# Edge features as two float32r parts, and the weight ring filled behind that stage

## The chip, the cores and the metric

The kernel runs on one core of one Trainium2 chip. The metric is the device time of one execution in microseconds. It stands at 4577.11 us, the median of three runs (4573.23 to 4581.51 us).

## The reference, cut to what matters

The program is four blocks over 512 nodes of 768 features and 8704 edges: in each a graph layer, an attention-like mixer and a feed-forward layer, and between them layer norms and residual sums. Only the first graph layer reads the edge features, a table of 8704 rows of 256 float32 values:

```python
edge_proj = edge_features @ We.T + be
for l in range(3):
    msgs = nodes[src] + nodes[dst] + edge_proj
    agg = jax.ops.segment_sum(msgs, dst, num_segments=512)
```

A sum over the edges of a node commutes with the product by `We`. So the kernel needs, for each node, the sum of the feature rows of the edges that end in it: a 256 x 512 matrix, `edge_sum_t`, at float32 accuracy.

## The kernel before

**The stage that the change touches.** Edges lie 128 on the partitions, in 68 chunks (`EC`). `edge_sum_t` is made by TensorE as a product of a chunk's features (128 edges x 128 features, the stationary operand) with a selection matrix (128 edges x 512 nodes, a one where the edge ends in the node), accumulated over all chunks in two PSUM banks, one for each half of the features. To keep float32 accuracy with bf16 operands each feature is split exactly into three bf16 parts, `feat_bits[...][:, 0..2, :]`: the value rounded to bf16, the rounded rest, and the rest of that.

Four chunks form a batch (`BATCHES` = 17). For a batch n:

- ScalarE writes part 0 (`first_bits`, L1440) and part 1 (L1446) and waits for VectorE's first subtraction between them (L1445).
- VectorE subtracts part 0 from the features (L2127, into `feat_rest`), builds the four selection matrices with one comparison each (L2132, a float16 iota against the edge's target, into `feat_hot`), and subtracts part 1 from the rest to give part 2 (L2134). It counts `onehot_ready` up by four there.
- TensorE waits for that count (L678) and runs 4 chunks x 2 halves x 3 parts = 24 matmuls of 512 columns (L683), and counts `onehot_used` up once a chunk.

`feat_bits` has three buffers, reused in order. `feat_hot` has two sets of four: the comparisons of batch n wait until batch n-2 is used (L2130, from n = 2). So VectorE is at most one batch ahead.

**Work put in between.** The first layer norm (`ln0`) runs inside this stage. On VectorE, behind the batch's last subtraction: one addition of two node chunks in batches 0 to 3 (L2042), small tables of edge kinds in batch 5 (L2107 to L2111), after a wait for TensorE's sum two centring steps in each of batches 6, 7 and 8 (L2144), a reciprocal in batch 13 (L2148), and two multiplications in each of batches 14, 15 and 16 (L2152). On TensorE: two float32 matmuls behind batch 5 (`norm_sums`) and six behind batch 10 (`square_sums`). On ScalarE: two squares in each of batches 7, 8 and 9 and a square root in batch 12. The order is the order of the code on each engine.

**What follows.** TensorE counts edges by kind in 6 groups of 34 chunks (L702, L703, L709, bf16), then does transposes (L539), degree sums (L541) and the first linear layer, which is the first reader of the weight ring.

**The SyncE queue** issues, in order: the node features and a column table, a wait until the second part of the edge features is in (L337), six weight tiles of 512 KB into the ring (L339), a wait for the fourth part of the edge features (L387), and `moe_pack` twice (L356 to L361), 34 transfers from HBM to HBM that repack expert weights for much later stages. Then come the ring's further tiles (L352), each waiting until its slot is free. ScalarE's queue issues the edges and the edge features, in four parts of 8, 16, 20 and 24 chunks.

The ring lies at `WR_`, 24 KB a partition. The buffers of the feature stage lie elsewhere, at `E_`, `D_`, `F_` and `T_`.

Of the kernel before, what the change touches and what calls it, by code (L numbers as in the profile page):

```python
# [23 lines left out]
N, D, P = 512, 768, 128  # L24
E, EC = 8704, 8704 // 128
# [28 lines left out]
BATCHES = EC // 4  # L54
# [63 lines left out]
def program(nc, io, tables):  # L118
    f32, bf16, f16, i32 = mybir.dt.float32, mybir.dt.bfloat16, mybir.dt.float16, mybir.dt.int32
    ALU, ACT, AX = mybir.AluOpType, mybir.ActivationFunctionType, mybir.AxisListType  # L120
    ctx = ExitStack()
    with ctx:
        def sb(name, shape, dt=f32):
            return ctx.enter_context(nc.sbuf_tensor(name, list(shape), dt))

        def sem(name):
            return ctx.enter_context(nc.semaphore(name))
# [2 lines left out]
        KB = 256  # L130
        CNT, A_, B_, C_, D_, XN_, T_, QK_, PQ_, XT_, WR_, E_, F_, END = (
            0, 32, 44, 56, 68, 80, 92, 108, 116, 124, 136, 160, 172, 184)
        mem = sb("mem", [P, END * KB])

        def area(kb, a, b, c=None, rows=P):
            size = a * b * (c or 1)
            v = mem[0:rows, int(kb * KB):int(kb * KB) + size]
            if c is None:
                return v.rearrange("p (a b) -> p a b", a=a)
            return v.rearrange("p (a b c) -> p a b c", a=a, b=b)  # L140
# [18 lines left out]
        edge_i = area(QK_ + 4, 4, EC).bitcast(i32)  # L159
        edge_f = area(QK_ + 5.25, 6, EC)  # L160
        feats = area(CNT, EC, 256)
        feat_hot = area(E_, 8, N // 2).bitcast(bf16)
        feat_bits = [area(kb, 3, 2 * 256).bitcast(bf16) for kb in (E_ + 8, D_, D_ + 6)]
        feat_rest = [area(kb, 4, 256) for kb in (F_ + 8, T_ + 12)]
        onehot_a = area(CNT + 12, AHEAD, N // 2).bitcast(bf16)
        onehot_b = area(A_, AHEAD, N // 2).bitcast(bf16)
        edge_sum_t = area(PQ_ + 4, 2, N)
# [84 lines left out]
        bank_full, bank_free, tile_free, x_tile_free, agg_done, act_done, dve_done, pool_done = (tally[n] for n in tally)  # L252
# [4 lines left out]
        feat_in = [sem(f"feat_in{i}") for i in range(4)]  # L257
        onehot_ready, onehot_used = sem("onehot_ready"), sem("onehot_used")
# [75 lines left out]
        def _(sp):  # L334
            sp.dma_start(XT, io["xT"]).then_inc(x_in, 16)
            sp.dma_start(cols[:, :], io["cols"]).then_inc(cols_in, 16)
            sp.wait_ge(feat_in[1], 16)  # L337
            for s in range(RING):
                sp.dma_start(ring[:, s, :], io["weights"][s]).then_inc(w_in[s], 16)  # L339

# [191 lines left out]
        def _(pe):  # L532
# [83 lines left out]
            def square_sums(label):  # L616
                for k in range(KC):
                    pe.wait_ge(act_done.sem, act_done.at((label, "sq", k)))
                    ins = mm(bank[6][:, :], ones[:, :], sq[:, k, :], k == 0, k == KC - 1, k == KC - 1)
                ins.then_inc(agg_done.sem, agg_done.tick((label, "var")))  # L620
# [56 lines left out]
            for n in range(BATCHES):  # L677
                pe.wait_ge(onehot_ready, 4 * n + 4)  # L678
                for b in range(4):
                    for f in range(2):  # L680
                        for part in range(3):
                            at = b * 256 + f * P
                            ins = nc.tensor.matmul(bank[4 + f][:, :], feat_bits[n % 3][:, part, at:at + P], feat_hot[:, n % 2 * 4 + b, :],  # L683
                                                   start=n == 0 and b == 0 and part == 0, stop=n == BATCHES - 1 and b == 3 and part == 2)
                    ins.then_inc(onehot_used, 1)
                if n == 5:
                    norm_sums("ln0", XT, lambda k: None)
                elif n == 10:
                    square_sums("ln0")
            for p in range(len(PACKED)):  # L690
                for g, (start, stop) in enumerate(GROUPS):
                    n = len(GROUPS) * p + g
# [11 lines left out]
                    for chunk in range(start, stop):  # L704
                        done = EC * p + chunk
                        a, b = onehot_a[:, done % AHEAD, :], onehot_b[:, done % AHEAD, :]
# [660 lines left out]
        def _(act):  # L1367
# [67 lines left out]
            def first_bits(n):  # L1435
                if n in [start // 4 for start, _ in FEAT_PARTS]:
                    act.wait_ge(feat_in[[start // 4 for start, _ in FEAT_PARTS].index(n)], 16)
                if n >= 3:
                    act.wait_ge(onehot_used, 4 * (n - 2))
                nc.scalar.activation(feat_bits[n % 3][:, 0, :], feats[:, 4 * n:4 * n + 4, :].rearrange("p a f -> p (a f)"),  # L1440
                                     ACT.Identity).then_inc(act_done.sem, act_done.tick(("first_bits", n)))

            first_bits(0)
            for n in range(BATCHES):
                act.wait_ge(dve_done.sem, dve_done.at(("feat_rest", n)))  # L1445
                nc.scalar.activation(feat_bits[n % 3][:, 1, :], feat_rest[n % 2].rearrange("p a f -> p (a f)"), ACT.Identity).then_inc(  # L1446
                    act_done.sem, act_done.tick(("middle_bits", n)))
                if n + 1 < BATCHES:
                    first_bits(n + 1)
                if n in (7, 8, 9):  # L1450
                    for k in (2 * n - 14, 2 * n - 13):
                        act.wait_ge(dve_done.sem, dve_done.at(("ln0", "d", k)))
                        nc.scalar.activation(sq[:, k, :], XN[:, k, :], ACT.Square).then_inc(act_done.sem, act_done.tick(("ln0", "sq", k)))
                elif n == 12:
                    act.wait_ge(agg_done.sem, agg_done.at(("ln0", "var")))
                    nc.scalar.activation(rstd[:, :], bank[6][:, :], ACT.Sqrt, scale=1.0 / D, bias=eps_col[:, :]).then_inc(
                        act_done.sem, act_done.tick(("ln0", "std")))
# [577 lines left out]
        def _(dve):  # L2035
            v = nc.vector

            def add_up(label, x, m):

                if 1 <= m < KC - 1:  # L2040
                    dve.wait_ge(dve_done.sem, dve_done.now())
                    v.tensor_tensor(mean[:, :], x[:, 0, :] if m == 1 else mean[:, :], x[:, m, :], ALU.add).then_inc(  # L2042
                        dve_done.sem, dve_done.tick((label, "part")))
# [71 lines left out]
            def key(n, c):  # L2115
                if isinstance(c, int):
                    return edge_f[:, n, c:c + 1]
                return edge_f[:, n, bass.ds(c, 1)]


            def flat(x):
                return x.rearrange("p a f -> p (a f)")

            for n in range(BATCHES):
                bits, rest = feat_bits[n % 3], flat(feat_rest[n % 2])
                dve.wait_ge(act_done.sem, act_done.at(("first_bits", n)))
                v.tensor_tensor(rest, flat(feats[:, 4 * n:4 * n + 4, :]), bits[:, 0, :], ALU.subtract).then_inc(  # L2127
                    dve_done.sem, dve_done.tick(("feat_rest", n)))
                if n >= 2:
                    dve.wait_ge(onehot_used, 4 * (n - 1))  # L2130
                for b in range(4):
                    v.tensor_scalar(feat_hot[:, n % 2 * 4 + b, :], iota_h, key(1, 4 * n + b), None, ALU.is_equal)  # L2132
                dve.wait_ge(act_done.sem, act_done.at(("middle_bits", n)))
                v.tensor_tensor(bits[:, 2, :], rest, bits[:, 1, :], ALU.subtract).then_inc(onehot_ready, 4)  # L2134
                if n == 0:
                    dve.wait_ge(x_in, 16)
                if n < 4:
                    add_up("ln0", XT, n + 1)
                elif n == 5:
                    edge_kinds()  # L2140
                elif n in (6, 7, 8):
                    dve.wait_ge(agg_done.sem, agg_done.at(("ln0", "sum")))
                    for k in (2 * n - 12, 2 * n - 11):
                        v.scalar_tensor_tensor(XN[:, k, :], bank[7][:, :], -1.0 / D, XT[:, k, :], ALU.mult, ALU.add).then_inc(  # L2144
                            dve_done.sem, dve_done.tick(("ln0", "d", k)))
                elif n == 13:
                    dve.wait_ge(act_done.sem, act_done.at(("ln0", "std")))
                    v.reciprocal(rstd[:, :], rstd[:, :]).then_inc(dve_done.sem, dve_done.tick("ln0_rstd"))  # L2148
                elif n > 13:
                    dve.wait_ge(dve_done.sem, dve_done.at("ln0_rstd"))  # L2150
                    for k in (2 * n - 28, 2 * n - 27):
                        v.tensor_tensor(XN[:, k, :], XN[:, k, :], rstd[:, :], ALU.mult).then_inc(dve_done.sem, dve_done.tick(("ln0", k)))  # L2152
# [28 lines left out]
            for p in range(len(PACKED)):  # L2181
                a, b_ = (0, 1) if p < 2 else (1, 0)
# [714 lines left out]
```

## Time and profile before

| | us |
|---|---|
| median of three runs | 4577.11 |
| lowest, highest | 4573.23, 4581.51 |
| span of the profiled execution, first to last instruction | 4586.8 |
| TensorE busy in it | 4400.9 (96%) |
| VectorE busy | 1028.0 (22%) |
| ScalarE busy | 1005.9 (22%) |

The profile gives no time of the profiled execution other than its span; that span lies 9.7 us above the median of the runs, 0.2%. Busy TensorE does not mean TensorE at its peak: matmuls are pipelined and their ends are modelled, so the distance from one start to the next is what a matmul costs, not its duration. A float32 matmul shows as two records. In the chain of waits, pieces with the name of a line are work on that line, and "issue" is time in which the engine waited for nothing that the profile shows.

### The profile page before, as it was taken

What the parts mean: (1) busy time and instruction counts of PE and PEld (TensorE: products, weight loads), DVE (VectorE), ACT (ScalarE), POOL (GpSimd) and SP (SyncE); (2) the same over time, 40 slices, a digit from 0 to 9 for tenths busy, and PEclk for the clock granted to TensorE, in tenths of its full rate; (3) what the DMA queues carried; (4) which work ended last, traced back from release to release, by engine and by line L of the source; (5) the groups of instructions that cost most, each with busy time, mean ns of one, the idle gap of its engine ahead of it and who ended that gap; (6) DMA issues with size and microseconds to landing.
All of it is one profiled execution on the core that took longest, in us unless ns stands there. A gap on an engine that the chain in (4) does not pass through costs nothing.

```text
span 4586.8 us, 37555 instructions
## 1 busy us (share of the span) xinstructions
PE 4400.9 (96%) x15153; PEld 1974.8 (43%) x15153; DVE 1028.0 (22%) x1909; ACT 1005.9 (22%) x1830; POOL 90.1 (2%) x169
## 2 busy tenths in 40 slices
PE   8999999999999998989999999999999999999998
PEld 3444444444445544444444444444444433433333
DVE  6871111212321325113300000023541000000000
ACT  3121122324214336222210101012621000110000
POOL 1000000000000000000000000000000000000000
PEclk9999999999999998999999999999899999999999
DMA  9513222111361120103203030355128999999998
GB/s 322 164 65 93 81 74 92 60 59 56 155 273 55 51 78 1 55 28 119 69 28 102 21 101 23 101 214 223 42 98 355 410 422 423 413 424 408 414 412 357
DMA packets 128791, 795.79 MB, mean 173 GB/s; under 512 B 13950, under 2 KB 26542, under 8 KB 82172
## 3 DMA queue, kind: packets, MB, share of 16 engines
q1 hardware_dynamic: 116892, 728.07, 42.2%
q0 software_dynamic: 9280, 45.81, 2.6%
q10 hardware_dynamic: 2464, 19.67, 1.1%
q8 instruction: 117, 1.92, 0.2%
q14 instruction: 38, 0.31, 0.0%
HBM read 774.47 MB, written 56.83 MB: 181 GB/s over the span
## 4 chain that ended last, share of the span: by engine, by line
PE 87%; DMA 5%; ACT 3%; DVE 3%; issue 1%; POOL 0%; SPq 0%; ACTq 0%; DVEq 0%; POOLq 0%
PE bank L541 78%; DMA mem<-in_experts 4%; PE bank L709 4%; PE bank L539 3%; PE bank L683 2%; ACT mem L1722 1%; ACT mem L1743 0%; ACT mem L1888 0%; DVE mem L2411 0%; DVE mem L2077 0%; DVE mem L2407 0%; ACT mem L1381 0%; ACT mem L1758 0%; DMA mem<-moe_up 0%; DMA mem<-moe_bias 0%
## 5 line engine op out<-in xcount | busy, mean ns | idle before, releaser
L541 PE MATMUL bank<-mem 128*128 128x512 f32 (+5 forms) x11160 | 3539.0, 557 | 51.5 <-DMA mem<-in_experts 25.1
L541 PEld LDWEIGHTS bank<-mem 128*128 128x128 f32 (+3 forms) x11160 | 1486.4, 167 | 2022.6 <-issue 1904.2
L539 PE MATMUL bank<-ident,mem 128*128 128x128 f32 (+2 forms) x1484 | 225.1, 303 | 73.1 <-ACT mem L1915 13.4
L539 PEld LDWEIGHTS bank<-ident,mem 128*128 128x128 f32 (+2 forms) x1484 | 188.5, 156 | 161.9 <-issue 87.8
L1381 ACT ACTIVATE mem<-bank 128x512 f32<-128x512 f32 x171 | 101.4, 596 | 511.3 <-PE bank L541 506.5
L1381 ACT ACTIVATE mem<-bank,cols 128x512 f32<-128x512 f32 (+1 forms) x82 | 56.2, 686 | 688.4 <-PE bank L541 688.4
L709 PE MATMUL bank<-mem 128*128 128x512 bf16 x816 | 177.2, 379 | 0.0
L2716 DVE TENSOR_TENSOR mem<-mem,EV 128x512 f32<-128x512 f32 x48 | 33.2, 692 | 549.2 <-ACT EV L1989 549.2
L541 PE MATMUL bank<-mem,ones 128*128 128x512 f32 (+1 forms) x314 | 141.9, 621 | 13.5 <-ACT mem L1415 7.2
L2694 DVE TENSOR_TENSOR mem<-mem,bank 128x512 f32<-128x512 f32 x48 | 33.0, 688 | 459.7 <-PE bank L541 459.7
L709 PEld LDWEIGHTS bank<-mem 128*128 128x128 bf16 x816 | 79.3, 98 | 97.5 <-issue 1.3
L2598 DVE COPY mem<-mem 128x512 f32<-128x512 f32 x12 | 4.2, 420 | 485.6 <-ACT mem L1381 485.6
L683 PE MATMUL bank<-mem 128*128 128x512 bf16 x408 | 90.9, 386 | 15.6 <-DVE mem L2134 15.6
L1989 ACT ACTIVATE EV<-bank 128x512 f32<-128x512 f32 x48 | 28.7, 597 | 310.9 <-PE bank L541 310.9
L1985 ACT ACTIVATE mem<-bank 128x512 f32<-128x512 f32 x48 | 28.7, 597 | 300.5 <-PE bank L541 300.5
L2090 DVE TENSOR_TENSOR mem<-mem,EV 128x512 f32<-128x512 f32 x30 | 20.8, 692 | 325.7 <-ACT EV L1392 325.7
L541 PEld LDWEIGHTS bank<-mem,ones 128*128 128x128 f32 (+1 forms) x314 | 55.7, 189 | 88.3 <-issue 56.6
L2187 DVE TENSOR_SCALAR mem<-mem 128x512 bf16<-128x512 f16 x204 | 82.5, 404 | 0.0
L1392 ACT ACTIVATE EV<-bank,cols 128x512 f32<-128x512 f32 x30 | 20.6, 687 | 279.1 <-PE bank L541 279.1
L2186 DVE TENSOR_SCALAR mem<-mem 128x512 bf16<-128x512 f16 x204 | 70.8, 347 | 29.6 <-PE bank L709 23.3
L1996 ACT ACTIVATE mem<-bank,pair_score 128x384 f32<-128x384 f32 x16 | 9.3, 581 | 275.1 <-PE bank L541 275.1
L2407 DVE SCALAR_TENSOR_TENSOR mem<-mem 128x2048 f32<-128x2048 f32 x27 | 61.8, 2287 | 33.8 <-ACT mem L1722 33.8
(364 smaller groups left out, 2147.9 us busy)
## 6 DMA issues: line engine op xcount, KB each, us to landing
mem<-in_experts SPq DMA_DIRECT2D x282, 1536.0 KB, 11.9
mem<-in_weights SPq DMA_DIRECT2D x329, 512.0 KB, 3.6
mem<-moe_up SPq DMA_DIRECT2D x30, 1152.0 KB, 9.0
mem<-moe_down SPq DMA_DIRECT2D x30, 1152.0 KB, 10.2
moe_up<-in_weights SPq DMA_DIRECT2D x16, 1152.0 KB
moe_down<-in_weights SPq DMA_DIRECT2D x16, 1152.0 KB
mem<-in_weights POOLq DMA_DIRECT2D x36, 384.0 KB, 7.8
mem<-in_experts ACTq DMA_DIRECT2D x6, 1536.0 KB, 15.3
```

Source lines behind the costliest of these rows:

```text
L539: ins = nc.tensor.transpose(out, lhsT, ident[0:lhsT.shape[0], 0:lhsT.shape[0]])
L541: ins = nc.tensor.matmul(out, lhsT, rhs, start=start, stop=stop)
L683: ins = nc.tensor.matmul(bank[4 + f][:, :], feat_bits[n % 3][:, part, at:at + P], feat_hot[:, n % 2 * 4 + b, :], start=n == 0 and b == 0 a ...
L709: ins = nc.tensor.matmul(banks[c][:, :], a[:, c * P:(c + 1) * P], b, start=False, stop=chunk == stop - 1)
L1381: nc.scalar.activation(dst(m), src[0:width, :], func, scale=scale, **how).then_inc(bank_free.sem, bank_free.tick((label, m)))
L1722: ins = nc.scalar.activation(scores[:, buf, t, :], src[:, :], ACT.Identity, bias=stat[:, at:at + 1])
L1985: nc.scalar.activation(x_hidden[:, b, :], src[:, :], ACT.Silu).then_inc(bank_free.sem, bank_free.tick((kind, p, b)))
L2186: v.tensor_scalar(onehot_a[:, done % AHEAD, :], iota_h, key(a, c), None, ALU.is_equal)
L2187: v.tensor_scalar(onehot_b[:, done % AHEAD, :], iota_h, key(b_, c), key(2 + p, c), ALU.is_equal, ALU.mult).then_inc(onehot_ready, 1)
L2407: v.scalar_tensor_tensor(wide, wide, 0.2, wide, ALU.mult, ALU.max).then_inc(dve_done.sem, dve_done.tick())
L2694: v.tensor_tensor(XT[:, m, :], XT[:, m, :], bank[7][:, :], ALU.add).then_inc(dve_done.sem, dve_done.tick(("experts_x", p, m)))
L2716: v.tensor_tensor(x_hidden[:, u // 2, :], x_hidden[:, u // 2, :], EV[:, u // 2 % 2, :], ALU.mult).then_inc(dve_done.sem, dve_done.tick(("x ...
```

## The change

The features are split into two float32r parts in place of three bf16 parts: the value rounded to float32r by ScalarE, and what is left of it, written by VectorE. The selection matrices are float32r too. All operands of L683 are then 4 bytes wide, and a batch has 16 matmuls. ScalarE's second conversion, VectorE's first subtraction and the buffer `feat_rest` go. The wider buffers take the ring's place (`WR_`, 24 KB) beside `E_` and `D_`, so the SyncE queue waits, before it fills the ring, until the whole stage is used (`onehot_used` at 68) and no longer for the second part of the features. All that SyncE issues behind the ring comes behind this wait as well.

```diff
-        feat_hot = area(E_, 8, N // 2).bitcast(bf16)
-        feat_bits = [area(kb, 3, 2 * 256).bitcast(bf16) for kb in (E_ + 8, D_, D_ + 6)]
-        feat_rest = [area(kb, 4, 256) for kb in (F_ + 8, T_ + 12)]
+        feat_hot = rounded("feat_hot", WR_, (8, N))
+        feat_bits = [rounded(f"feat_bits{n}", kb, (2, 4 * 256)) for n, kb in enumerate((WR_ + 16, E_, D_))]
...
-            sp.wait_ge(feat_in[1], 16)
+            sp.wait_ge(onehot_used, EC)
             for s in range(RING):
                 sp.dma_start(ring[:, s, :], io["weights"][s]).then_inc(w_in[s], 16)
...
-                        for part in range(3):
+                        for part in range(2):
                             at = b * 256 + f * P
                             ins = nc.tensor.matmul(bank[4 + f][:, :], feat_bits[n % 3][:, part, at:at + P], feat_hot[:, n % 2 * 4 + b, :],
...
-            first_bits(0)
             for n in range(BATCHES):
-                act.wait_ge(dve_done.sem, dve_done.at(("feat_rest", n)))
-                nc.scalar.activation(feat_bits[n % 3][:, 1, :], feat_rest[n % 2].rearrange("p a f -> p (a f)"), ACT.Identity).then_inc(
-                    act_done.sem, act_done.tick(("middle_bits", n)))
-                if n + 1 < BATCHES:
-                    first_bits(n + 1)
+                first_bits(n)
...
             for n in range(BATCHES):
-                bits, rest = feat_bits[n % 3], flat(feat_rest[n % 2])
-                dve.wait_ge(act_done.sem, act_done.at(("first_bits", n)))
-                v.tensor_tensor(rest, flat(feats[:, 4 * n:4 * n + 4, :]), bits[:, 0, :], ALU.subtract).then_inc(
-                    dve_done.sem, dve_done.tick(("feat_rest", n)))
+                bits = feat_bits[n % 3]
                 if n >= 2:
                     dve.wait_ge(onehot_used, 4 * (n - 1))
                 for b in range(4):
                     v.tensor_scalar(feat_hot[:, n % 2 * 4 + b, :], iota_h, key(1, 4 * n + b), None, ALU.is_equal)
-                dve.wait_ge(act_done.sem, act_done.at(("middle_bits", n)))
-                v.tensor_tensor(bits[:, 2, :], rest, bits[:, 1, :], ALU.subtract).then_inc(onehot_ready, 4)
+                dve.wait_ge(act_done.sem, act_done.at(("first_bits", n)))
+                v.tensor_tensor(bits[:, 1, :], flat(feats[:, 4 * n:4 * n + 4, :]), bits[:, 0, :], ALU.subtract).then_inc(onehot_ready, 4)
```

`rounded` is a new helper that places a float32r tensor at a fixed offset in the same memory.

## Rows read from the trace of the kernel before

**Rows 1.** The page: the span, and the chain that ended last, by engine and line.
```profile
span 4586.8 us, 37555 instructions
...
PE 87%; DMA 5%; ACT 3%; DVE 3%; issue 1%; POOL 0%; SPq 0%; ACTq 0%; DVEq 0%; POOLq 0%
PE bank L541 78%; DMA mem<-in_experts 4%; PE bank L709 4%; PE bank L539 3%; PE bank L683 2%; ACT mem L1722 1%; ACT mem L1743 0%; ACT mem L1888 0%; DVE mem L2411 0%; DVE mem L2077 0%; DVE mem L2407 0%; ACT mem L1381 0%; ACT mem L1758 0%; DMA
```

**Rows 2.** The chain in order of time, 0 to 330 us: start, length, what.
```profile
10.64 1.06 ACT mem L1440
...
11.80 1.23 DVE mem L2127
13.03 1.15 DVE mem L2132 x4
...
14.22 1.24 DVE mem L2134
...
15.59 33.55 PE bank L683 x144
49.13 1.72 PE bank L541 x4
50.85 25.90 PE bank L683 x120
76.75 5.15 PE bank L541 x12
81.90 31.08 PE bank L683 x144
112.98 0.32 PE bank L702
...
300.70 1.75 PE bank L539 x16
302.45 13.73 PE bank L541 x32
```

**Rows 3.** Groups of instructions, 0 to 114 us: busy, mean ns, idle before.
```profile
L683 PE MATMUL bank<-mem 128*128 128x512 bf16 x408 | 90.9, 386 | 15.6 <-DVE mem L2134 15.6
```

**Rows 4.** Timeline inside the stage, TensorE and VectorE: start, length, what.
```profile
50.69 9.66 PE L683 MATMUL bank<-mem 128*128 128x512 bf16 x44
50.89 1.29 DVE L2144 SCALAR_TENSOR_TENSOR mem<-bank,mem 128x512 f32<-128x512 f32 x2 [4.46 <-PE bank L541]
52.10 1.21 DVE L2127 TENSOR_TENSOR mem<-mem 128x1024 f32<-128x1024 f32 x1
...
71.61 1.14 DVE L2132 TENSOR_SCALAR mem<-mem 128x512 bf16<-128x512 f16 x4 [1.67 <-PE bank L683]
72.67 1.22 DVE L2134 TENSOR_TENSOR mem<-mem 128x1024 bf16<-128x1024 f32 x1
...
89.31 3.35 DVE L2148 RECIPROCAL rstd<-rstd 128x512 f32<-128x512 f32 x1
92.57 1.16 DVE L2127 TENSOR_TENSOR mem<-mem 128x1024 f32<-128x1024 f32 x1
```

**Rows 5.** Timeline of VectorE around 814 us, a float32 operation with a per-partition operand.
```profile
814.44 1.67 DVE L2240 TENSOR_SCALAR mem<-mem,stat 128x512 f32<-128x512 f32 x4
```

**Rows 6.** Timeline of SyncE's queue, 0 to 175 us.
```profile
15.78 2.81 SPq L339 DMA_DIRECT2D mem<-in_weights  x6
...
35.30 0.73 SPq L359 DMA_DIRECT2D moe_up<-in_weights  x1
...
168.94 1.25 SPq L361 DMA_DIRECT2D moe_bias<-in_weights  x1
```

**Rows 7.** Windows: us, length, busy PE, PEld, DVE, ACT, POOL, granted clock, DMA share, GB/s.
```profile
180.00:185.00 5.00, 5.00 (x25) 2.26 (x24) 3.95 (x12) 2.21 (x2) 0.00 (x0) 1.00 0.11 41
...
3216.00:3220.00 4.00, 1.26 (x10) 0.84 (x9) 3.54 (x6) 4.00 (x12) 0.00 (x0) 1.00 0.42 131
3220.00:3224.00 4.00, 4.00 (x10) 1.80 (x10) 2.90 (x15) 4.00 (x9) 0.00 (x0) 0.75 0.00 0
```

More of the change, by code:

```diff
@@ L132, in program, with rounded @@
             0, 32, 44, 56, 68, 80, 92, 108, 116, 124, 136, 160, 172, 184)
+        mem_at = -(-nc.sbuf_base // 32) * 32
         mem = sb("mem", [P, END * KB])
+        f32r = mybir.dt.float32r
+        def rounded(name, kb, shape, rows=P):
+            return nc.alloc_sbuf_tensor_at(name, [rows] + list(shape), f32r, offset=mem_at + int(kb * 1024))
         def area(kb, a, b, c=None, rows=P):
@@ L680, in _ @@
                     for f in range(2):
-                        for part in range(3):
+                        for part in range(2):
                             at = b * 256 + f * P
                             ins = nc.tensor.matmul(bank[4 + f][:, :], feat_bits[n % 3][:, part, at:at + P], feat_hot[:, n % 2 * 4 + b, :],
-                                                   start=n == 0 and b == 0 and part == 0, stop=n == BATCHES - 1 and b == 3 and part == 2)
+                                                   start=n == 0 and b == 0 and part == 0, stop=n == BATCHES - 1 and b == 3 and part == 1)
                     ins.then_inc(onehot_used, 1)
```

## The prediction

> **What bounds the kernel now.** I read the page first, for the chain that ended last: TensorE holds 87% of it, and the lines of the feature stage little of that, 2% for L683 [rows 1]. So the change can move a few tens of microseconds of 4577 and no more, and the stage has to be read by itself. Second, the chain in order of time over the first 330 us [rows 2]. The reader is to see that it has one head (ScalarE's first conversion, VectorE's subtraction, four comparisons, second subtraction) and from 15.59 us on only TensorE: 408 matmuls of L683 in three pieces, with 4 and 12 records of the layer norm between them, and at 112.98 the counting stage, without a piece of another engine. Third, the groups: L683's only idle time, 15.6 us, is the head [rows 3]. The stage is bound by TensorE's stream, and VectorE and ScalarE hide behind it. Fourth, VectorE's and SyncE's timelines, for what the change turns into a bound [rows 4 to 6].
>
> **Part by part.**
>
> *Matmuls.* The last two pieces give 25.90/120 and 31.08/144, both 0.2158 us from one matmul to the next [rows 2]. The first piece has 144 as well and took 33.55, so the slow start of TensorE costs 2.47; I keep that. The change drops 136 of 408 matmuls. If a float32r matmul of 512 columns costs what a bf16 one does, 136 x 0.2158 = 29.35 us go.
>
> No float32r matmul is in the trace. Below, its price is bounded by the bf16 one: as many columns pass through. Above, the nearest row is float32: 32 records in 13.73 us, 0.429 each, two records to a matmul, so 0.858 a matmul [rows 2]. That is four times 0.2146, the pace of a bf16 matmul. Four is what the products of two halves by two halves make, and an operand that is not cut in halves needs one. So I take 0.2158. It also says that 4-byte operands can be streamed at that pace. The weight load is no obstacle: float32 records of 128 columns follow each other by 1.75/16 = 0.109 us with a load each [rows 2], so a 4-byte load fits within 0.216. The ends for the range are 0.2158 and 0.429 (0.858 for the extreme that float32r runs as float32).
>
> The Trainium skill (FP8 and Floating Point Precision, TensorE Precision Notes) says that true float32 takes four passes and that there is a reduced form which reads 4-byte values and truncates them. Its four passes agree with 0.858 = 4 x 0.2146; that the reduced form takes one pass it does not say in so many words, and no run so far shows it. By one pass the stage's matmuls would be an estimated 272 x 0.2146 = 58.4 us, by four 233 us.
>
> *The head.* Before, the first matmul starts at 15.59, after L1440, L2127, L2132 and L2134 in a row. After the change the comparisons stand ahead of the wait for ScalarE and need only the edges, which VectorE has long before 10.64. Left are L1440 and one subtraction, which starts at 11.80 where L2127 did, and takes 1.23; with the 0.14 from 15.45 (14.22 plus 1.23, as I read its end) to 15.59 TensorE starts at 13.17. That is 2.42 us earlier.
>
> *VectorE for a batch.* Comparisons before: from 71.61 to the subtraction's start at 72.67, 1.06 for four, 0.265 each [rows 4]. Their output becomes 4 bytes wide. The nearest row is the float32 operation with a per-partition operand: four in 1.67, the last one lasting 0.48, so (1.67 - 0.48)/3 = 0.397 each, 1.59 for four [rows 5]. Bounds: 0.265 if the width costs nothing; above, 1.22 for 1024 elements of L2127 against about 0.69 for 512 says 0.53 more for 512 elements at one a cycle, and 0.397 had 256 steps' worth, so 0.397 + 0.267 = 0.66 each, 2.66 for four, if a 2-byte source with a 4-byte result falls to one element a step. I take 1.59: the row has the result's width and the source costs less. The subtraction stays at 1.22; its rows with bf16 and with float32 results are alike (L2134 and L2127) [rows 4].
>
> The Trainium skill (VectorE: DVE Perf Modes, The perf-mode tier table) speaks against the change here: 4 elements a cycle only for 2-byte operands in SBUF, 2 for float32. That is 128 against 256 cycles, an estimated 0.133 us more for each comparison; the rows' 0.397 - 0.265 = 0.132 agrees.
>
> VectorE may begin batch n+1 when batch n-1 is used, which is when TensorE starts batch n. From there: 0.20 us until VectorE runs (TensorE's next matmul started at 50.69, VectorE's L2144, which waited for the one before, at 50.89), 1.59, 1.22, and 0.14 to TensorE: 3.15 [rows 4]. TensorE's batch is 16 x 0.2158 = 3.45. In plain batches 0.30 us are to spare; before, VectorE idled 1.67 in front of the comparisons at 71.61.
>
> Now the layer norm's work, which was hidden in that reserve. It stands between two batches on VectorE, and the next instruction starts 0.09 before the last ends. One addition (0.60, half of the 1.21 for two in [rows 4]) starts 0.23 before TensorE's batch (0.14 and 0.09) and lets the comparisons begin at 0.37 in place of 0.20; the reserve covers that, four times. The kinds' tables of batch 5 fall beside the two float32 matmuls. Then:
> - batch 6: VectorE waits for the sum, 0.20, and centres two chunks, 1.21 (50.89 to 52.10), then 1.59 + 1.22 + 0.14 = 4.36 against 3.45: a stall of 0.91.
> - batches 7 and 8: -0.23 + 1.21 + 1.59 + 1.22 + 0.14 = 3.93: 0.48 each.
> - batch 13: the reciprocal, 3.26 (89.31 to 92.57): -0.23 + 3.26 + 2.95 = 5.98, less 3.45, less the 0.30 that VectorE is ahead: 2.23.
> - batches 14 and 15: two multiplications, priced like the centring steps: 0.48 each. Batch 16's lie behind the last batch.
> The stalls sum to 5.06 us. ScalarE now has one conversion of 1.06 for a batch and at most 1.2 of squares beside it, in 3.45 to 4.4: it is not late.
>
> *Sum.* TensorE starts at 13.17; 272 x 0.2158 = 58.70; slow start 2.47; layer norm 1.72 + 5.15; stalls 5.06: the stage ends at 86.3 instead of 112.98. The saving is 29.35 + 2.42 - 5.06 = 26.7 us. From 112.98 to 316 the chain is TensorE alone, so it carries over whole.
>
> *SyncE.* The wait moves from 15.8 to about 86.3. Behind it queue the six ring tiles and the 34 transfers of `moe_pack`, whose wait for the features is then met. Issuing them took from 15.78 to 18.59 and from 35.30 to 170.19, 134.9 us [rows 6]; they would be issued by 86.3 + 2.8 + 134.9 = 224, and the transfers, which die out by 185, 15 us after the last issue [rows 7], by 239. The first reader of the ring is the linear layer, at 316 (302.45 plus 13.73) less 27 = 289, and SyncE's next tile waits for that layer [rows 2]: 50 us are left, and the ring itself is in by about 115 at the worst. The cost is nothing, and it would begin to cost only if the transfers took 1.4 times as long. The features lose a competitor: their last part, in by 35.3, is wanted in batch 11, at 62. That gains nothing either, since nothing waited for it.
>
> **The profiled execution and the median.** The sum is made against the span, 4586.8 - 26.7 = 4560.1. The profiled run lies 9.7 us above the median; I take the same saving off the median: 4577.1 - 26.7 = 4550.4 us.
>
> **Rivals.**
>
> *A, the forecast*, 4550: chance 0.68. Its own range is 4545 to 4558, from comparisons at 0.265 each (the stalls shrink to 1.5 us, 3.5 more saved) to a clock that falls in the 2.23 us stall. For the latter the trace has a case: after 4 us in which TensorE was busy for 1.26 the granted clock read 0.75 [rows 7]; at half speed a batch costs 3.45 more, and one or two would.
>
> *B, VectorE becomes the bound.* Comparisons at 0.66 each make 0.20 + 2.66 + 1.22 + 0.14 = 4.22 in a plain batch, 0.77 over TensorE's, and the extra work finds no reserve at all. By the same steps the stalls are 0.77 four times, 0.94 twice, 0.40, 1.58, 1.55 four times and 3.60, 16.7 in place of 5.1. Saving 15.1: 4562. For it: a float16 source with a 4-byte result is not in the trace. Against it: no row of a dense comparison or copy ran at one element a step. Chance 0.11.
>
> *C, slower: a float32r matmul costs one float32 record, 0.429.* It decides at 0.333: there 272 matmuls are as long as the old 408 (88.05) and the head's 2.42; the stalls vanish as TensorE slows. At 0.429 the matmuls take 116.7, nothing stalls (a batch is 6.9), and the saving is 88.05 - 116.7 + 2.42 = -26.2: 4603. For it: two records to a float32 matmul may mean that the hardware's unit for 4-byte operands is the record. Against it: the record has twice the time of a pass. The extreme, float32r run as float32, gives 88.05 - 233.4 + 2.42 = -142.9: 4720. Chance 0.09 for both, 0.02 of it the extreme: that is also the case in which the change doesn't do what it says.
>
> *D, the 4-byte weight load isn't hidden.* If a load of 0.109 [rows 2] were added to each matmul, 0.325 each, the matmuls take 88.3, without stalls, and the saving is 88.05 - 88.3 + 2.42 = 2.2: 4575. Against it: the float32 records of 512 columns keep 0.429, twice 0.2146, with a load each, so there it is hidden. Chance 0.06.
>
> *E, the gain is taken back behind the stage*: `moe_pack` beside the counting stage down to its end, late tiles, or another wait. Before, the same transfers ran beside this stage until 185 and no TensorE idle time stands there; a loss of half would give 4564. Chance 0.06.
>
> **Range and chances.** What one measurement tells from no change here is 0.2%, 9 us. Leaving out C (0.09), D (0.06) and a little of A's lower edge, the range is 4541 to 4569. Faster by over 0.2% (below 4568): A, B and E, 0.85. Within 0.2%: D, 0.06. Slower: C, 0.09.
>
> **What would show it.** L683 has 272 matmuls, one record each, 0.216 from start to start, and the last ends near 86. VectorE's four comparisons span about 1.6 to the subtraction. TensorE waits for the subtraction's line six times, 5.1 us in all, the longest 2.2 before batch 14. The counting stage is 187.7 long as before, and SyncE's last `moe_pack` issue is at about 221. I am wrong in the price if the distance is 0.3 or 0.43, wrong about VectorE if plain batches stall, and wrong about the carry-over if the stage ends at 86 and the whole does not follow.

## The result, and the profile after

| | before | after |
|---|---|---|
| median of the first comparison, us | 4579.24 | 4553.62 |
| ratio, 95% interval | | 0.9942 (0.9930 to 0.9954) |
| median of a second comparison, us | 4580.02 | 4554.53 |
| ratio, 95% interval | | 0.9941 (0.9928 to 0.9955) |
| span of the profiled execution, us | 4586.8 | 4550.0 |
| its own time, us | not given | 4551.79 |
| feature stage ends at, us | 112.98 | 88.51 |

The change makes the kernel faster by 25.6 us, where 26.7 were forecast. The spans of the two profiled executions lie 36.8 apart, which is more than the medians do: single executions of one kernel differ by some 12 us (4545.26 to 4557.60 after), so the question of where the time came from is answered in the stage and not by the spans.

The forecast was 4550.4 us, counted from a median before of 4577.11; the first comparison has 4579.24 before, so 2.1 of the 3.2 us between forecast and result come from the kernel before. The interval allows a saving of 21 to 32 us, so the whole's time can't tell 26.7 from the 24.5 that the stage shows below.

The page of the kernel after, its span and the chain that ended last:

```profile
span 4550.0 us, 37248 instructions
...
PE 87%; DMA 5%; ACT 3%; DVE 3%; issue 1%; SPq 0%; POOL 0%; ACTq 0%; DVEq 0%; POOLq 0%
PE bank L545 79%; DMA mem<-in_experts 4%; PE bank L713 4%; PE bank L543 3%; PE bank L687 1%; ACT mem L1721 1%; DMA mem<-moe_up 0%; ACT mem L1742 0%; ACT mem L1887 0%; DVE mem L2407 0%; DVE mem L2076 0%; DVE mem L2403 0%; ACT mem L1385 0%; ACT mem L1757 0%; DMA mem<-y_by_slot,slot_i 0%
```

TensorE holds 87% of the chain as it did [rows 1]. The share of the feature matmuls (L683 before, L687 now) has moved from 2% to 1%; the other large shares are the same within 1%. The chain over the first 300 us, as start, length and what:

```profile
10.66 1.07 ACT feat_bits L1444
11.82 1.24 DVE feat_bits L2130
...
13.19 24.42 PE bank L687 x96
37.61 1.73 PE bank L545 x4
...
39.97 0.68 DVE mem L2140
40.65 1.86 DVE feat_hot L2128 x4
42.51 1.14 DVE feat_bits L2130
43.70 15.42 PE bank L687 x64
59.12 5.15 PE bank L545 x12
64.27 3.69 PE bank L687 x16
...
70.79 0.85 DVE rstd L2144
...
73.97 1.30 DVE feat_hot L2128 x4
...
76.74 7.84 PE bank L687 x32
84.58 3.92 PE bank L687 x16
88.51 0.32 PE bank L706
...
276.23 1.75 PE bank L543 x16
277.98 13.73 PE bank L545 x32
```

Beside [rows 2] three things are to be seen. The head has lost a subtraction and the comparisons, and TensorE starts at 13.19, not at 15.59. VectorE's lines now stand inside the stage, where the chain was TensorE alone: at 40 us (centring, comparisons, subtraction) and at 71 us (the reciprocal and what follows it). And from the stage's end on nothing changed: 276.23 - 88.51 = 187.72, before 300.70 - 112.98 = 187.72, and the linear layer behind it still begins 15.5 us later. The stage gave 24.47 us and all of it arrived at the linear layer. The chains of both kernels have the same distance 480 us further on (first line before, second line after):

```profile
796.82 10.31 PE bank L541 x24
772.35 10.31 PE bank L545 x24
```

796.82 - 772.35 = 24.47. Behind 950 us it wanders in steps up and down, to 36.8 at the end of these two executions. These steps are not traced to a cause; the medians, 25.6 apart, don't keep them.

The groups of the stage (busy and mean ns of one, then idle before):

```profile
L687 PE MATMUL bank<-feat_hot,feat_bits 128*128 128x512 f32 x272 | 67.3, 406 | 15.4 <-DVE feat_bits L2130 15.4
L2128 DVE TENSOR_SCALAR feat_hot<-mem 128x512 fp32r<-128x512 f16 x68 | 28.9, 487 | 11.7 <-PE bank L687 11.5
```

and who waited for whom in the first 95 us (total, times, longest):

```profile
PEld bank L687 <- DVE feat_bits L2130: 4.7, 6, 2.0
```

A float32r matmul is one record, as forecast. TensorE's weight loads wait for the subtraction's line six times, 4.7 us in all, the longest 2.0; six times, 5.1 and 2.2 were forecast. This is idle time of the weight loads; what the matmuls lost is counted below.

The price of one matmul does not stand in its duration (406 ns, against 386 before [rows 3]) but in the distance of starts. The timeline of the weight loads up to the end of batch 5 (the last two loads of batch 2 and batches 3 to 5, where nothing stalls) has a row that gives it:

```profile
25.89 11.29 PEld L687 LDWEIGHTS bank<-feat_hot,feat_bits 128*128 128x128 f32 x50
```

The last of the 50 loads takes 0.195 (0.19 in the rows of single ones), so (11.29 - 0.195)/49 = 0.2264 us from one to the next. For bf16 it was 0.2158. VectorE's timeline, a plain batch and the reciprocal's:

```profile
30.39 1.68 DVE L2128 TENSOR_SCALAR feat_hot<-mem 128x512 fp32r<-128x512 f16 x4 [0.82 <-PE bank L687]
31.98 1.22 DVE L2130 TENSOR_TENSOR feat_bits<-mem,feat_bits 128x1024 fp32r<-128x1024 f32 x1
...
70.71 3.35 DVE L2144 RECIPROCAL rstd<-rstd 128x512 f32<-128x512 f32 x1
73.97 1.58 DVE L2128 TENSOR_SCALAR feat_hot<-mem 128x512 fp32r<-128x512 f16 x4
```

The comparisons take 31.98 - 30.39 = 1.59 to the subtraction, the value that was taken, and the 1.67 us that VectorE idled ahead of them [rows 4] are 0.82. SyncE's queue after:

```profile
88.54 2.81 SPq L343 DMA_DIRECT2D mem<-in_weights  x6
...
219.95 2.03 SPq L365 DMA_DIRECT2D moe_bias<-in_weights  x1
```

All that stood from 15.78 to 170.19 [rows 6] stands from 88.54 to 221.98. The linear layer, the ring's first reader, starts at 277.98 + 13.73 = 291.7, 70 us behind the last issue.

### The profile page after: what moved, and what is told of

Same layout as the page of the kernel before. It is cut to its first block, busy times and chain, and to the rows that moved or that the text cites. A ratio compares the mean times of both kernels' runs of the same rounds, so it can differ in the third digit from the quotient of the medians.

```text
span 4550.0 us, 37248 instructions
## 1 busy us (share of the span) xinstructions
PE 4371.0 (96%) x15017; PEld 1985.1 (44%) x15017; DVE 1017.1 (22%) x1892; ACT 990.1 (22%) x1813; POOL 92.0 (2%) x169
## 4 chain that ended last, share of the span: by engine, by line
PE 87%; DMA 5%; ACT 3%; DVE 3%; issue 1%; SPq 0%; POOL 0%; ACTq 0%; DVEq 0%; POOLq 0%
PE bank L545 79%; DMA mem<-in_experts 4%; PE bank L713 4%; PE bank L543 3%; PE bank L687 1%; ACT mem L1721 1%; DMA mem<-moe_up 0%; ACT mem L1742 0%; ACT mem L1887 0%; DVE mem L2407 0%; DVE mem L2076 0%; DVE mem L2403 0%; ACT mem L1385 0%; ACT mem L1757 0%; DMA mem<-y_by_slot,slot_i 0%
## 5 line engine op out<-in xcount | busy, mean ns | idle before, releaser
L713 PE MATMUL bank<-mem 128*128 128x512 bf16 x816 | 177.2, 379 | 0.0
L687 PE MATMUL bank<-feat_hot,feat_bits 128*128 128x512 f32 x272 | 67.3, 406 | 15.4 <-DVE feat_bits L2130 15.4
L2407 DVE CUSTOM_DVE_ANT_0 mem<-mem 128x512 f32<-128x512 f32 x108 | 68.3, 688 | 0.9
```

The lines of the kernel that those rows point to most:

```text
L713: ins = nc.tensor.matmul(banks[c][:, :], a[:, c * P:(c + 1) * P], b, start=False, stop=chunk == stop - 1)
L2407: v.tensor_tensor_reduce(out=s, in0=s, in1=cnt[r][:, t, :], scale=1.0, scalar=-3e38, op0=ALU.add, op1=ALU.max, accum_out=top[:, t, r:r + 1 ...
```

## The experiments

Each kernel below was compared with the kernel before on the same chip. Ahead of them, the account that they test, from the chain after: 88.51 - 13.19 = 75.32 us of stage are 272 x 0.2264 = 61.58 of matmuls, 6.88 of layer norm matmuls, a slow start of 24.42 - 96 x 0.2264 = 2.7, and 4.2 of stalls, which is what is left.

**The changed kernel again.** No edit.

> The changed kernel once more, beside the others on one chip. Theory: 0.994 of the kernel before (25 us less), the feature stage ends at 88.5. If the saving were chance between executions, it would lie under 9 us here.

Measured: 0.9941 (0.9928 to 0.9955), 4554.53 against 4580.02 us. Its stage ends at 88.54. The saving repeats.

**SyncE's wait alone.**

```diff
-            sp.wait_ge(feat_in[1], 16)
+            sp.wait_ge(onehot_used, EC)
             for s in range(RING):
```

> The kernel before with one part of the change alone: SyncE's wait ahead of the weight ring stands on the end of the feature stage, so the six ring tiles and the 34 repacking transfers are issued from about 113 us on. My theory (that move costs and gives nothing): the feature stage still ends at 113.0, the counting stage still takes 187.7, the last repacking transfer is issued at about 113 + 135 = 248, 70 us ahead of the first linear layer at 302 + 14 = 316, and the time is that of the kernel before within 0.1%. Rival (traffic out of the feature stage is what helps, or traffic in the counting stage is what hurts): the stage ends earlier than 113, or the counting stage takes more than 188, or the first linear layer waits, and the time moves by 3 us or more.

Measured: 1.0008 (0.9998 to 1.0017), 4582.08 against 4580.02 us. Its chain:

```profile
49.75 1.72 PE bank L541 x4
...
113.60 0.32 PE bank L702
...
301.32 1.75 PE bank L539 x16
```

The counting stage takes 301.32 - 113.60 = 187.72, to the hundredth what it took without the transfers moved into it. The stage ends 0.6 later, and that lies in its start: its first 144 matmuls took 49.75 - 15.56 = 34.19, of which 3.1 are a slow start, against 2.47 [rows 2]. SyncE's last repacking issue ends at 247.7, 69 us ahead of the linear layer at 316.8. So the move neither costs nor gives anything in the traced stages. The whole's interval doesn't exclude a cost of up to 0.17%, 8 us; nothing in the trace up to the linear layer shows one.

**Two parts, but bf16.** Leaves the third part of each feature out.

```diff
-        f32r = mybir.dt.float32r
+        f32r = mybir.dt.bfloat16
```

> The changed kernel with bf16 in the place of float32r, in features and selection matrices: two bf16 parts, so the third part of each feature is left out. All else is as in the changed kernel: 272 matmuls, the same order, the same waits. It takes away the two things that a 4-byte operand costs. Theory: a matmul goes back from 0.2266 to 0.2158 us from start to start (2.9 us in all), the four comparisons from 1.59 to 1.06, so that of 4.3 us of stalls 1.5 are left; the feature stage ends at 82.8. If the 0.2266 came from the order or from what VectorE and ScalarE do beside it, and not from the type, the matmuls stay at 0.2266 and the stage ends at 85.7.

Measured: 0.9945 (0.9927 to 0.9963), 4550.53 against 4579.35 us. Its chain, and the weight loads of its plain batches:

```profile
35.56 1.73 PE bank L545 x4
...
81.74 0.32 PE bank L706
```

```profile
20.08 14.99 PEld L687 LDWEIGHTS bank<-feat_hot,feat_bits 128*128 128x128 bf16 x70
```

The stage ends at 81.74, 6.8 us ahead of float32r. (14.99 - 0.10)/69 = 0.2158: with the same order, the same waits and the same engines beside it the matmul is back at the bf16 pace. The comparisons are back at 1.05 (51.47 to 52.52 in its timeline). The account closes: 81.74 - 13.22 = 68.52 are 58.70 + 6.88 + 1.6 of slow start + 1.3 of stalls. So the type of the operands costs 2.9 us in matmuls and 2.9 in stalls; the remaining 1.1 of the 6.8 are a shorter slow start. Why that is shorter here is not shown; it differs without a known cause between the other kernels too (last section).

**Cut into halves and quarters.**

```diff
+                            pieces = 1 if n in (0, BATCHES - 1) else 2
+                            for q in range(pieces):
+                                own = slice(q * N // pieces, (q + 1) * N // pieces)
-                            ins = nc.tensor.matmul(bank[4 + f][:, :], ..., feat_hot[:, n % 2 * 4 + b, :],
+                                ins = nc.tensor.matmul(bank[4 + f][:, own], ..., feat_hot[:, n % 2 * 4 + b, own],
```

with 4 in the place of 2 for quarters.

> The changed kernel with each float32r matmul of batches 1 to 15 cut into two of 256 columns, with a weight load each. It asks what the extra 0.011 us of a float32r matmul is. If it grows with the columns (0.2266/512 a column): 0.1133 each, a plain batch stays at 3.63. If it is a fixed addition to each matmul (0.2133 for the columns and 0.013): 0.120 each, a plain batch of 3.84. If the 4-byte weight load, recorded at 0.195, is what binds: 0.19 to 0.23 each, a plain batch of 6.2 to 7.2, and the stage ends past 125. I hold the fixed addition likeliest.

> The same with four matmuls of 128 columns. By columns: 0.0567 each, a plain batch of 3.63. By a fixed addition of 0.013: 0.0665 each, 4.26 a batch. By a weight load that can no longer hide: the float32 records with 128 columns kept 0.109, so 0.109 each if the load sets it, 7.0 a batch. I expect the load to show here whatever the halves show: 0.09 to 0.11 each.

Measured in one execution each. The weight loads' timeline for the halves, then for the quarters with the chain's last piece of their stage:

```profile
27.84 9.91 PEld L690 LDWEIGHTS bank<-feat_hot,feat_bits 128*128 128x128 f32 x82
```

```profile
25.83 29.11 PEld L690 LDWEIGHTS bank<-feat_hot,feat_bits 128*128 128x128 f32 x260
```

```profile
97.74 39.40 PE bank L690 x336
```

256 columns: (9.91 - 0.19)/81 = 0.1200. 128 columns: (29.11 - 0.19)/259 = 0.1117. From 512 to 256 columns the distance falls by 0.2264 - 0.1200 = 0.1064, so about 0.0136 of it did not go with the columns. An addition that grows with them (0.1132 for 256) is out, and so is the load as the bound at 512 and 256, since it let 0.1117 pass. At 128 columns it is another thing: half of 0.1064 and 0.0136 would be 0.067, and 0.112 came, so there the 4-byte load, or something else that each matmul pays once, is the bound. The stage of the quarters ended at 137.1 (97.74 plus 39.40), and the whole took 4601.19 us; the halves' took 4553.81.

**Float32 in one part.** Needs no split; the conversions still run beside it.

```diff
-        f32r = mybir.dt.float32r
+        f32r = mybir.dt.float32
...
+                            if part == 0:
-                                ins = nc.tensor.matmul(bank[4 + f][:, :], feat_bits[n % 3][:, part, at:at + P], ...
+                                ins = nc.tensor.matmul(bank[4 + f][:, :], feats[:, 4 * n + b, f * P:(f + 1) * P], ...
```

> Features as they are, in float32, in one part: 136 matmuls of float32 operands, two records each, with a float32 selection matrix; the conversions still run beside it. It prices the form that needs no split. By the rows of the kernel before, 0.858 a matmul: 136 x 0.858 = 116.7 us of matmuls and the layer norm's 6.9 with a slow start of 2.5, so that the stage ends near 139 and the whole is 26 us above the kernel before. It is what my rival C would have been for float32r.

Measured in one execution: 4607.33 us, 28 above the kernel before. The chain's last piece of the stage:

```profile
98.25 41.22 PE bank L688 x96
```

0.4294 a record, two records to each of its 48 matmuls, and the stage ends at 139.5. A record's 0.429 is the price that rival C gave to one float32r matmul. Two float32r matmuls, 0.453, take the place of one float32 matmul of 0.859.

**Three sets of selection matrices.**

```diff
-        feat_hot = rounded("feat_hot", WR_, (8, N))
-        feat_bits = [... enumerate((WR_ + 16, E_, D_))]
+        feat_hot = rounded("feat_hot", WR_, (12, N))
+        feat_bits = [... enumerate((E_, E_ + 8, D_))]
...
-                if n >= 2:
-                    dve.wait_ge(onehot_used, 4 * (n - 1))
+                if n >= 3:
+                    dve.wait_ge(onehot_used, 4 * (n - 2))
```

and `n % 3` for `n % 2` where `feat_hot` is read and written.

> The changed kernel with three sets of selection matrices in place of two, so that VectorE may be two batches ahead of TensorE. Theory (the six stalls come from VectorE being held to one batch ahead while the layer norm's work stands in its order): the stall of 2 us before batch 14 and those of batches 15 and 16 go, of those behind batch 6 some 1.3 us stay because VectorE waits there for TensorE's sum, and the feature stage ends at 85.2 to 85.8 in place of 88.5. Rival (a float32r matmul has another irregular cost that only looks like stalls): the stage ends at 88 as before. The whole moves with the stage, 3 us, 0.07%, which is at the edge of what five rounds can tell.

Measured: 0.9946 (0.9933 to 0.9960), 4553.76 us, against 4554.53 of the changed kernel in the same comparison: not to be told apart. Its chain at the start and behind the square sums:

```profile
13.35 23.42 PE bank L687 x96
...
57.98 5.15 PE bank L545 x12
63.12 21.82 PE bank L687 x96
```

The last six batches are one piece of 21.82 = 96 x 0.2273, with the reciprocal and the multiplications behind it; in the changed kernel they took 88.51 - 64.27 = 24.24. The stage ends at 84.94. Of the 3.6 us less, 1.0 is a shorter slow start, offset by a start 0.16 later, and 2.7 are stalls: 1.4 are left of 4.2. So 2.7 us of the stalls came from VectorE being held to one batch ahead, as the theory has it; the 1.4 that stay lie between the two layer norm pieces, in batches 6 to 10, where VectorE first waits for TensorE's sum.

**All three edits.** Beside the sets, the centring steps a batch later, and TensorE busy before the first batch.

```diff
-                elif n in (6, 7, 8):
+                elif n in (7, 8, 9):
...
+            pe.wait_ge(pool_done.sem, pool_done.at("consts"))
+            for _ in range(20):
+                nc.tensor.matmul(bank[7][:, 0:P], ones[:, :], ident[:, :], start=True, stop=True)
             pe.wait_ge(x_in, 16)
-            pe.wait_ge(pool_done.sem, pool_done.at("consts"))
```

with ScalarE's squares in batches 8, 9 and 10.

> The changed kernel with three more things: three sets of selection matrices; the centring steps of the layer norm one batch later on VectorE (batches 7, 8 and 9) and the squares one batch later on ScalarE, so that VectorE has a batch ready before it waits for TensorE's sum; and 20 matmuls of constants on TensorE before the first batch, so that its slow start falls in time in which it had nothing to do. Theory: no stalls are left (4.3 us) and the slow start's 2.5 us go: TensorE's stage lasts 272 x 0.2266 + 6.9 = 68.5 from 13.2, so it ends at 81.7 to 82.5, and the whole is 6 us below the changed kernel, 31 us below the one before. Rival: the clock does not stay up through the hand-over at 13 us, and the stage ends at 84 to 84.5.

Measured: 0.9933 (0.9919 to 0.9946), 4549.86 us. Its timeline of TensorE, and its chain:

```profile
5.82 7.66 PE L681 MATMUL bank<-ident,ones 128*128 128x128 f32 x40 [5.82 <-POOL ident L437]
```

```profile
13.48 21.78 PE bank L689 x96
35.26 1.72 PE bank L545 x4
36.98 18.18 PE bank L689 x80
55.16 5.15 PE bank L545 x12
60.31 21.82 PE bank L689 x96
```

The first 96 matmuls take 21.78 in place of 24.42: 0.2269 each, no slow start. The first of them starts at 13.24 in the timeline, against 13.19 in the changed kernel, so the twenty matmuls of constants did not hold it up. All pieces are TensorE's and touch one another; the stage ends at 82.13, 6.4 ahead of the changed kernel. By the medians of one comparison it is 4.7 us ahead of it, where 6 were expected, and 30 us ahead of the kernel before. The two intervals against the kernel before overlap, so that 4.7 rests on the stage's trace and not on the timing alone.

## Why the prediction was right, step by step

- **Matmuls.** The count was right, and so was one record for each matmul. The price was 0.2158 and is 0.2264: the term of the sum that was mis-sized. 136 matmuls fewer gave 29.35 by the forecast; 88.05 - 61.58 = 26.5 is what came. The 2.9 us are shown to belong to the type (they go with bf16 operands in the same order), 0.011 a matmul. Halving the columns shows an addition to each float32r matmul that doesn't shrink with them; bf16 matmuls were not halved. What in the hardware adds it stays open. The argument for one pass began with a rounding: 0.858 / 4 = 0.2146 was called the pace of a bf16 matmul, which is 0.2158 in the same rows; that 0.5% decided nothing, but the step from there to 0.2158 for float32r left out any cost of its own. The Trainium skill (FP8 and Floating Point Precision, TensorE Precision Notes) says four passes for true float32 and names a reduced 4-byte form. The trace agrees with the first, 0.859 against four times 0.2158 = 0.863; for the second it shows 0.2264, near one pass, which the page does not state.
- **The head.** 13.17 forecast, 13.19 measured.
- **Comparisons.** 1.59 forecast from a float32 row, 1.59 measured: the float16 source with a 4-byte result costs what the float32 row did, 0.397 each, and not rival B's 0.66. The step that the change pays for on VectorE was sized rightly, and rival B fell with it. The Trainium skill (VectorE: DVE Perf Modes, The perf-mode tier table) has `tensor_scalar` at four times the base rate for bf16 in SBUF and at twice for float32, and no column for a 2-byte source with a 4-byte result. The trace puts that mixed form with float32, 0.397 against 0.265 us each.
- **Stalls.** Six, at the places named; 5.06 forecast, about 4.2 measured. They are smaller because the matmuls are slower: a batch of 16 x 0.2264 = 3.62 leaves VectorE 0.17 more in each. The reserve and the two hand-overs were forecast at 0.30 + 0.34 = 0.64 of idle time in a plain batch; with 0.17 more that is 0.81, and 0.82 is in the trace. Three sets took 2.7 of them away, which shows the cause of those.
- **Slow start and layer norm.** 2.47 and 6.87 kept; 2.7 and 6.88 measured.
- **SyncE.** Cost nothing that the traces show, by its part alone. The last issue was forecast to end at 224 and ended at 222, and that is closer than its terms: the stage ended 2.2 later than forecast, and the repacking issues took 130.6 us (91.39 to 221.98) and not 134.9.
- **Carry-over.** The counting stage is 187.72 in both and the distance is still 24.47 at 797 us, so rival E fell.
- **The sum.** 26.7 forecast; the stage gave 24.5 and the medians 25.6. Two errors with one cause, +2.9 and -0.9, and a slow start 0.2 longer make the difference in the stage. That the medians' 25.6 lies nearer to 26.7 than the stage's 24.5 does is chance, since they can't resolve 2 us. Rivals C and D fell with the distance of starts: the edge between a gain and a loss lay at 0.333 a matmul.

## What to carry to other kernels

Float32 sums against a 0/1 matrix cost two float32r matmuls of 0.226 us for 512 columns, against three of 0.216 in bf16 or one of 0.859 in float32 (no run here measures how exact each of the sums is); the two wider operands are paid on VectorE, where each comparison with a 4-byte result takes 0.397 us and not 0.265. When a change takes a third of the bound engine's work out of a loop, go through every instruction that stood in the other engine's reserve: here the layer norm's steps, free before, came back as 4 us of stalls, and one more set of buffers removed most of them. A timing that can't resolve 3 us can be replaced by the end of the stage in the trace, as long as what follows is shown to be unchanged and the slow start, which differed by up to 1.5 us between these traces, is taken out first.

## What the runs showed of the hardware that was not expected

- A float32r matmul takes 0.2264 us at 512 columns and 0.1200 at 256 from start to start, so 256 columns cost 0.1064 and about 0.0136 comes with each matmul. A bf16 matmul of 512 columns takes 0.2158; if its columns cost the same, 0.003 comes with each. With 128 columns a float32r matmul with its load took 0.112.
- TensorE has a slow start. In the trace of the kernel before, two weight loads inside it, and the window around them (its last three numbers are the granted clock, the DMA share and GB/s):

```profile
18.10 0.15 PEld L683 LDWEIGHTS bank<-mem 128*128 128x128 bf16 x1 [0.28 <-issue]
18.53 0.15 PEld L683 LDWEIGHTS bank<-mem 128*128 128x128 bf16 x1 [0.27 <-issue]
...
18.00:20.00 2.00, 2.00 (x6) 0.76 (x5) 1.86 (x3) 1.22 (x2) 1.81 (x4) 1.00 0.97 409
```

Starts lie 0.43 apart and not 0.216, half the pace, though the granted clock reads 1.00 there, its upper level of 2.4 GHz; TensorE had done nothing before 15.59. The slow start cost 2.5 us in the kernel before, 3.1 in the one with SyncE's wait moved, 2.7 in the changed kernel in both of its traces, 1.7 with three sets and 1.6 with bf16. What makes the difference stays open: with one or two traces of each kernel it is not shown whether it goes with the kernel or with the execution. Twenty small matmuls ahead of the stage (7.7 us of otherwise idle time) took it away in the one trace of that kernel.
